# An audio tower of eight rows: setup waits moved in the opening, a weight in four parts, slot indices in one step, and the ending's calls in another order

## The reference, cut to what matters

```python
h = gelu(features @ W1 + b1)                       # 128 -> 512
h = gelu(h @ W2 + b2)                              # 512 -> 512
new_lens = sigmoid((h @ W3 + b3)[..., 0])
new_lens = new_lens / sum(new_lens, axis=1, keepdims=True) * (Tq / FACTOR)
Xnew = warp_weights(cumsum(new_lens)) @ features   # 750 -> 375 tokens

h = h + attention(layernorm(h))                    # q: softmax over channels, k: over tokens

logits = xf @ switch_w.T + switch_b                # xf = layernorm(h), 3000 tokens
route_probs = max(softmax(logits)); routes = argmax(softmax(logits))
pos = cumsum(one_hot(routes), axis=0)[routes] - 1
keep = pos < capacity                              # 225
y = einsum('ecd,efd->ecf', buf, expert_w) + expert_b
out = where(keep, y[routes, pos], xf) * route_probs
h = h + out
```

## Time and profile before

| | |
|---|---|
| median of 3 runs | 397.14 us (396.93 to 398.03) |
| the profiled execution | 397.55 us, of which the span of the engines' work is 395.8 |
| PE busy | 374.6 us (95%), 2706 products |
| DVE busy | 331.1 us (84%), 897 instructions |
| ACT busy | 227.5 us (57%), 432 |
| POOL busy | 142.0 us (36%), 191 |
| granted clock of PE | 0.997 of full speed |

### The profile page before, as it was taken

The page is one execution under the profiler, slowest core; times in us unless marked ns, Lnnn a source line. Parts: engine busy times, 40 slices in busy tenths (PEclk is TensorE's granted clock), DMA queues, the critical chain, the costliest instruction groups (busy, mean ns, idle before and its releaser), DMA issues. The chain is left out here.

```text
span 395.8 us, 7949 instructions
## 1 busy us (share of the span) xinstructions
PE 374.6 (95%) x2706; PEld 326.0 (82%) x2706; DVE 331.1 (84%) x897; ACT 227.5 (57%) x432; POOL 142.0 (36%) x191
## 2 busy tenths in 40 slices
PE   7889989999999999999999999999999989999992
PEld 7667868898888889888888888888888778998892
DVE  3587759969897998889898989798998974988896
ACT  4633448915992499339943895279637743683200
POOL 6101110122168215831484038413840611106880
PEclk9999999999999999999999999999999999999998
DMA  7796002100200030002000200100000052241135
GB/s 220 192 228 235 2 1 55 30 2 3 84 2 20 3 84 2 21 1 84 2 18 5 84 2 11 58 1 1 17 7 0 9 144 69 70 131 31 40 83 127
DMA packets 16358, 21.58 MB, mean 55 GB/s; under 512 B 4882, under 2 KB 11880, under 8 KB 15886
## 3 DMA queue, kind: packets, MB, share of 16 engines
q1 hardware_dynamic: 12350, 18.30, 16.6%
q0 software_dynamic: 2880, 2.35, 2.5%
q10 hardware_dynamic: 1088, 0.42, 0.4%
HBM read 14.40 MB, written 6.62 MB: 53 GB/s over the span
## 5 line engine op out<-in xcount | busy, mean ns | idle before, releaser
L1081 PE MATMUL psB<-W2h,h1l 128*125 128x512 f32 x192 | 77.9, 406 | 2.0 <-DVE h2b L1623 1.3
L1082 PE MATMUL psB<-W2l,h1h 128*125 128x512 f32 x192 | 75.6, 394 | 0.0
L1083 PE MATMUL psB<-W2h,h1h 128*125 128x512 f32 x192 | 75.6, 394 | 0.0
L681 ACT ACTIVATE h2b<-h2b 125x512 f32<-125x512 f32 x48 | 30.1, 628 | 32.9 <-DVE h2b L1623 32.5
L1081 PEld LDWEIGHTS psB<-W2h,h1l 128*125 128x125 f32 x192 | 35.6, 185 | 9.9 <-issue 1.8
L1083 PEld LDWEIGHTS psB<-W2h,h1h 128*125 128x125 f32 x192 | 35.6, 185 | 8.9
L1082 PEld LDWEIGHTS psB<-W2l,h1h 128*125 128x125 f32 x192 | 35.7, 186 | 7.2
L670 ACT ACTIVATE h<-psA,b1c 128x376 f32<-128x376 f32 x64 | 35.4, 579 | 8.4 <-PE psA L1052 8.1
L1623 DVE TENSOR_TENSOR h2b<-psB,b2r 125x512 f32<-125x512 f32 x48 | 32.8, 686 | 8.0 <-PE psB L1083 7.8
L596 POOL DMA_INDIRECT slot_x<-xf,idx_s x18 | 32.5, 1807 | 7.8 <-issue 7.8
L1630 DVE CUSTOM_DVE_ANT_0 h2b<-h2b,W3r 125x512 f32<-125x512 f32 x48 | 32.9, 691 | 1.7 <-ACT h2b L681 1.4
(11 more groups left out here) (266 smaller groups left out, 967.8 us busy)
## 6 DMA issues: line engine op xcount, KB each, us to landing
xTf<-in_x_t SPq DMA_DIRECT2D x16, 187.5 KB, 2.6
xt<-in_x SPq DMA_DIRECT2D x8, 336.0 KB
slot_x<-eb_parts SPq DMA_DIRECT2D x2, 960.0 KB, 13.5
basef<-in_L_tok_W SPq DMA_DIRECT2D x1, 1024.0 KB, 6.9
ewT<-in_expert_t SPq DMA_DIRECT2D x1, 1024.0 KB, 9.3
ewf<-slot_x SPq DMA_DIRECT2D x2, 480.0 KB, 6.1
h2b<-slot_x SPq DMA_DIRECT2D x2, 480.0 KB, 8.5
slot_y<-h SPq DMA_DIRECT2D x4, 240.0 KB, 2.5
```

What stands on the lines that cost most here:

```text
L681: nc.scalar.activation(slot, slot, ACT.Gelu).then_inc(c_g2.sem, 1)
L1081: mm(ps, lo, W2h[:, k, :], start=k == 0, stop=False)
L1082: mm(ps, hi, W2l[:, k, :], start=False, stop=False)
L1083: last = mm(ps, hi, W2h[:, k, :], start=False, stop=k == HK - 1)
```

## The change

**The opening.** PE has 12 warm-up products for 14. The first layer-1 products of row 0 no longer wait until W1l is there: PE does W1h·xTl and W1h·xTh, and waits only for W1l·xTh. Row 0's layer 1 uses six banks, so that a call waits for a GELU of ACT only from the seventh on. W2 comes in four transfers with a semaphore each; DVE splits each quarter as it lands, and h1 of the first half is split in two pairs of hidden blocks. The first two layer-2 blocks are made in halves (`layer2_first`): both over hidden blocks 0 and 1, then both over 2 and 3.

```diff
+        def bank_l1(b, n):
+            return psC[n - 2] if row_is(b, 0) and 2 <= n < 6 else psA[n % 2]
...
-        WARM_UP = 14
+        WARM_UP = 12
...
-            sp.dma_start(W2f, W2.rearrange("(k p) n -> p k n", p=128)).then_inc(s_w2, 16)
+            for k in range(HK):
+                sp.dma_start(W2f[:, k, :], W2[k * 128:(k + 1) * 128]).then_inc(s_w2[k], 16)
...
             def layer1(b, prev, i, k):
...
-                if n >= 2:
+                if prev is None:
+                    if n >= 6:
+                        after(pe, c_g1, b, n - 5)
+                elif n >= 2:
                     after(pe, c_g1, b, n - 1)
...
+                if prev is None and i == 0 and k % 2 == 0:
+                    pe.wait_ge(s_prep, 1)
+                    mm(ps, W1h[:, w], xTl[:, i, :], start=True, stop=False)
+                    mm(ps, W1h[:, w], xTh[:, i, :], start=False, stop=False)
+                    pe.wait_ge(s_prep, 2 + k // 2)
+                    mm(ps, W1l[:, w], xTh[:, i, :], start=False, stop=True).then_inc(c_l1.sem, 1)
...
+            def layer2_first(j, ks):
+                _, cols = half_cols(j)
+                for k in ks:
+                    pe.wait_ge(s_w2l, k + 1)
+                    if k < 2:
+                        pe.wait_ge(s_h1l, 1)
+                    else:
+                        after(pe, c_h1l, 0, 1)
+                    hi, lo = h1h[:, k, 0, cols], h1l[:, k, 0, cols]
+                    ps = psB[j][0:TP, :]
+                    mm(ps, lo, W2h[:, k, :], start=k == 0, stop=False)
+                    mm(ps, hi, W2l[:, k, :], start=False, stop=False)
+                    last = mm(ps, hi, W2h[:, k, :], start=False, stop=k == HK - 1)
...
-            dve.wait_ge(s_w2, 16)
-            vec.tensor_copy(W2h[:], W2f).then_inc(s_prep, 1)
-            dve.wait_ge(s_prep, 4)
-            vec.tensor_tensor(W2l[:], W2f, W2h[:], ALU.subtract).then_inc(s_prep, 1)
+            for pair in range(2):
+                for k in (2 * pair, 2 * pair + 1):
+                    dve.wait_ge(s_w2[k], 16)
+                    vec.tensor_copy(W2h[:, k, :], W2f[:, k, :]).then_inc(s_w2h, 1)
+                    dve.wait_ge(s_w2h, k + 1)
+                    vec.tensor_tensor(W2l[:, k, :], W2f[:, k, :], W2h[:, k, :], ALU.subtract).then_inc(s_w2l, 1)
+                ks = slice(2 * pair, 2 * pair + 2)
...
+                vec.tensor_tensor(h1l[:, ks, 0, :], h1[:, ks, 0, :], h1h[:, ks, 0, :], ALU.subtract).then_inc(s_h1l if pair == 0 else c_h1l.sem, 1)
```

```diff
             def opening():
-                h1_lower(0, None, 0)
                 x_lo_next(0)
                 bias2(0, None, 0)
                 bias2(0, None, 1)
                 h1_lower(0, None, 1)
-                setup()
                 bias2(0, None, 2)
-                bias2(0, None, 3)
                 dot3(0, None, 0)
                 dot3(0, None, 1)
+                bias2(0, None, 3)
+                h1_lower(1, 0, 0)
+                scale_weights()
+                bias2(0, None, 4)
...
                 lengths(0, None)
                 warp_weights(0, None)
+                split_weights()
```

```diff
                after(dve, c_pp, b, 2)
...
+                if not ends(b):
+                    if prev is not None:
+                        after(dve, c_sct, prev, 48)
+                    vec.scalar_tensor_tensor(idx_s[:], pos[:], float(E), rm[:], ALU.mult, ALU.subtract).then_inc(c_idx.sem, 1)
+                    after(dve, c_idx, b, 1)
+                    vec.tensor_scalar(idx_g[:, bass.ds(b * GJ, GJ)], idx_s[:], float(SLOTS - 1), None, ALU.min).then_inc(c_idx.sem, 1)
```

```diff
                 scan(LAST, PRIOR)
-                query_norm(PRIOR, PRIOR - 1)
                 lengths(LAST, PRIOR)
                 warp_weights(LAST, PRIOR)
```

More of the change, by code:

```diff
@@ L426, in _ @@
             load_turned(1, 0)
-            sp.wait_ge(s_w2, 16)
+            for k in range(HK):
+                sp.wait_ge(s_w2[k], 16)
             load_tokens(0, None)
@@ L2119, in ending @@
-                query_sum(PRIOR, PRIOR - 1)
-                bias2(LAST, PRIOR, 5)
+                key_max(PRIOR, PRIOR - 1, 3)
                 dot3(LAST, PRIOR, 4)
+                keep_h(PRIOR, PRIOR - 1)
                 dot3(LAST, PRIOR, 5)
-                key_max(PRIOR, PRIOR - 1, 3)
                 scan(LAST, PRIOR)
-                query_norm(PRIOR, PRIOR - 1)
                 lengths(LAST, PRIOR)
                 warp_weights(LAST, PRIOR)
+                query_sum(PRIOR, PRIOR - 1)
@@ L2128, in ending @@
+                key_sum(PRIOR, PRIOR - 1)
+                query_norm(PRIOR, PRIOR - 1)
+                moments1(LAST, PRIOR)
                 probability(PRIOR - 1, PRIOR - 2)
-                key_sum(PRIOR, PRIOR - 1)
-                moments1(LAST, PRIOR)
+                normal1(LAST, PRIOR)
+                xn_lo(LAST, PRIOR)
                 take_m(PRIOR, PRIOR - 1)
-                normal1(LAST, PRIOR)
+                keep_base(PRIOR - 1, PRIOR - 2)
+                query_max(LAST, PRIOR, 0)
@@ L2144, in ending @@
                 key_max(LAST, PRIOR, 1)
                 key_max(LAST, PRIOR, 2)
+                query_sum(LAST, PRIOR)
                 take_logits(PRIOR, PRIOR - 1)
+                take_outputs(5)
                 key_max(LAST, PRIOR, 3)
                 route(PRIOR, PRIOR - 1)
-                take_outputs(5)
-                query_sum(LAST, PRIOR)
+                spread_choice(PRIOR)
+                keep_h(LAST, PRIOR)
+                query_norm(LAST, PRIOR)
                 take_outputs(7)
@@ L2165, in ending @@
                 own_tokens(PRIOR, 5)
-                out_norm(LAST, PRIOR)
+                take_m(LAST, PRIOR)
                 own_tokens(PRIOR, 6)
@@ L2192, in ending @@
                 finish_row(PRIOR)
+                place_in_expert(LAST, PRIOR)
                 own_tokens(LAST, 5)
```

313 lines of the change are left out of this document (143 added, 170 removed).

## The result

The changed kernel took **394.51 us** (median; 394.20 to 394.68), the kernel before 397.58 beside it: a ratio of 0.9923, 95% interval 0.9903 to 0.9942, or 3.1 us less. I had forecast 390.5, 6.6 less. The sign was right and the time lies inside the wide range of 387 to 395, but the gain is less than half of the one that I forecast. The profiled execution took 394.20 us, its span is 392.5, where it was 395.8.

A forecast was written before the change was run, and what follows sets the result against it. The opening was taken to wait on PE's suppliers, the middle to be full on PE, the ending bound by PE and DVE handing each other work. 4.9 + 0 + 1.8 = 6.7 off 397.14 gave 390.5 us, range 388 to 392, with rivals 387 to 395.

The forecast's parts named there:

- the opening (4.9): First 52 us: earlier layers 1 and 2 and setup moved behind the biases give a lead of 4.9 us.
- rivals 1 and 2: Opening: W2's pieces come late (392.1 us, chance 0.09), or each pays its start anew (392.4 us, chance 0.04).
- The middle (0): Looped steps: nine small POOL operations fewer and two DVE operations more per slot row change the time by 0.
- The ending (1.8): Behind the loop: the new order of DVE's calls brings 1.8 us.
- about 1.9 us of waits: Ending, until LAST's last dot product: two formerly covered POOL powers make DVE wait about 1.9 us.
- the walk: Ending: DVE's calls added up in the new order; lead 3.6 us at LAST's xn, only 0.6 at its context.
- a wait of PE at `chosen_on_rows(PRIOR)`: Ending, ahead of LAST's query transposes: PE stands some 1.6 us until place_in_expert(PRIOR) is done.
- rivals 4 and 5: Ending: gathers end last, 398.5 us, chance 0.04; middle: something due at a fixed time returns the lead, 395.5 us, 0.05.
- Rival 3: Ending: waits eat the new order's gain, so it gives nothing; 393.2 us (392 to 394.5), chance 0.18.

The follow-up runs named there:

- w2_whole: The changed kernel with W2 loaded by one transfer and split by DVE in one cast and one subtraction; 401.34 us.
- scatter_split: sum_beside_power with the first of a row's three scatter transfers issued ahead of POOL's power, the other two behind it; 392.49 us.
- sum_beside_power: The changed kernel with query_sum moved behind minus_z, beside POOL's power for PRIOR, and query_norm behind scan; 393.11 us.
- opening_only: The kernel before with only the changed kernel's opening, indices on POOL and the ending's order as before; 393.57 us.

## Why the prediction was wrong

**What bounds the kernel, and the opening (4.9): right.** Layer 1 started at 6.19 (forecast 5.9), layer 2 at 10.59 (10.15), a quarter of W2 takes 1.06 us of DVE (1.05), and blocks 2 to 5 of row 0 start at 18.21, 21.51, 24.29 and 27.07, each 0.3 or 0.4 later than forecast, which is the later start. (The end of the four half blocks in my sum, 15.95, should have been 16.0.) PE's longest wait from 6 to 33 us is 0.2, so nothing there waits for setup. Block 5 is 4.55 ahead and `sums` 4.62. Of this 0.44 goes at row 0's normalization, where dx stood still beside a dot product and took 2.08 (1.64 in the kernel before), so 4.18 of the 4.9 remain. Setup has a share in that: its split ended at 41.79 and not at 41.4, 0.46 behind ACT's copy, which was to cover it (41.33). With it the dot product slipped to the start of dx (43.52 and 43.56, where the kernel before has 47.69 and 48.18).

The pieces of W2 came in time, and rivals 1 and 2 fell:

```profile
6.86 0.41 DVE L2243 CAST W2h<-basef 128x512 fp32r<-128x512 f32 x1
7.31 0.69 DVE L2245 TENSOR_TENSOR W2l<-basef,W2h 128x512 fp32r<-128x512 f32 x1
7.92 0.42 DVE L2243 CAST W2h<-basef 128x512 fp32r<-128x512 f32 x1
```

No cast waits for its transfer. The Trainium skill, DMA: Bandwidth & Descriptors, section Bandwidth, speaks for large transfers, and w2_whole has one; there the cast waits 1.62 us for it, and the time is 7 us longer. How much of the 7 is the transfer's own is not shown, as that run splits W2 in one piece too.

**The middle (0): 0.5 lost,** the end of the bound that was given, but by another way. The two operations of DVE cost nothing that shows: scatter_split has them and keeps its lead. What was not seen is that POOL, rid of nine operations, issues its transfers earlier, and the third falls on `warp_weights`. I had counted what leaves POOL, and not what then moves up.

**The ending (1.8): this is the step that failed.** From row 5's xn to the end, 3.67 becomes 3.3 of span: a loss of 0.4. The prediction added up "what DVE has to do in the new order, each call at its duration in the timeline". At the duration that it had beside `query_sum`, 1.33, PRIOR's power would have ended at 274.27, under the cover of `query_norm` (to 274.51), and cost no wait. It took 2.77 there, and DVE waited 1.23. The "about 1.9 us of waits" for two powers does not say which two; DVE's waits for POOL from 272 to 319 are now 1.23, 1.01 (`norm1`) and 0.42 (`normal2`).

How much that step cost is seen by taking the lead at row 5's xn as zero. Each number is the lead at that place less the lead at row 5's xn, in us.

| place | forecast | changed kernel | sum_beside_power | scatter_split |
|---|---|---|---|---|
| LAST's `scan` | +0.4 | -0.84 | +0.34 | +0.35 |
| LAST's xn transposed | +3.6 | +1.69 | +2.87 | +2.89 |
| LAST's `context` | +0.6 | -1.61 | -0.45 | -0.43 |
| LAST's selections, first | +1.8 | -0.46 | +0.70 | +0.71 |

Of the 2.2 us missing in this term, 1.2 are gone by LAST's `scan`, and with the power beside `query_sum` the scan comes as forecast. So half of the miss is this one step. Of the 1.1 that is still missing then, 0.7 goes between the scan and xn. There the scan's first operation takes 0.60 for the 0.17 of the kernel before, 0.43 more, beside the third transfer of the scatter (the rows are the changed kernel's; scatter_split has 0.60 too):

```profile
314.63 1.73 POOL L578 DMA_INDIRECT slot_x<-xf,idx_s  x1 [0.30 <-issue]
315.73 0.60 DVE L1661 TENSOR_SCALAR sg<-sg 125x6 f32<-125x6 f32 x1 [0.45 <-ACT sg L736]
```

That is the same step failing once more: a call at its old duration beside a new neighbour. The rest, some 0.7, stays open.

From xn to `context` the lead is given back nearly as forecast (3.3 us, where the walk had 3.0), but not for the reason that the prediction gave, which was DVE and a wait of PE at `chosen_on_rows(PRIOR)`. That wait did not come. PE is full from LAST's xn to `context`, in the kernel before (first row) and in the changed one, and it now has 3.2 us more to do there, above all PRIOR's `fold` and `attend`, which have come behind xn (from 330.06 and 331.60 to 329.84 and 332.33):

```profile
334.73:356.06 21.33, 21.33 (x163) 19.69 (x161) 19.32 (x60) 15.86 (x44) 2.80 (x6) 1.00 0.31 93
329.37:354.00 24.63, 24.55 (x197) 22.36 (x196) 20.66 (x61) 14.93 (x42) 4.34 (x6) 1.00 0.23 68
```

The columns are those of the earlier trace rows. Moving xn ahead of work that PE has to do all the same brings `context` nothing; the forecast had its size right by luck.

That rivals 4 and 5 were unlikely was right: the gathers are issued from 356.72 to 385.15, and DVE comes to the last rows at 387.14 without a wait; opening_only shows that the opening's lead is not given back. Rival 3, the ending gives nothing, is what happened. The time is 1.3 us above the 393.2 that it gave: the opening fell short by 0.7 and the middle lost 0.5, while the ending lost 0.4 and not 1; and the kernel before took 397.58 beside it, not 397.14. The sign that was given for it, DVE idle for more than 3 us from 272 to 319, is in the profile (47 - 40.06 = 6.9), but the kernel before had 47 - 42.90 = 4.1 there, so that sign could not tell them apart. Its chance of 0.18 was too low, and 0.60 for a walk of over a hundred calls without a measured row for one new neighbourhood was too high. (The chances of 0.91 and 0.05 count rival 5 as "same" alone, though the prediction splits it.)

**It stood in the trace of before.** In a looped step of the kernel before, one small operation of POOL beside `query_norm` takes 1.75 us where its neighbours take 0.20:

```profile
113.16 0.20 POOL L583 TENSOR_TENSOR place<-place,tok 125x3 f32<-125x3 f32 x1
...
113.39 1.75 DVE L1738 SCALAR_TENSOR_TENSOR qa<-qa,rq 125x1536 f32<-125x1536 f32 x1
113.44 1.75 POOL L585 TENSOR_TENSOR place<-place,keep 125x3 f32<-125x3 f32 x1
```

I had summed the nine operations as small and gone by.

## What to carry to other kernels

When calls are put in a new order, look not only at what each waits for, but at what runs beside it on the engine that shares a path with it: in the trace of the old order, search for the same operation at two durations and see what stood beside the long one. Cover is not all alike: beside a reduction POOL's power took its usual 1.33 us, beside a product of two operands in on-chip memory twice that. And work that is taken off an engine lets the rest of its queue move up; follow that queue to where it lands.
